# Products that nobody reads in TensorE's row, in the front of the first routed layer

## The reference

```
z = (x - mu) * rsqrt(var + EPS) * ln_g + ln_b          # layer norm of a layer norm of x
z_bn  = (mean over tokens of z - bn_mean) * rsqrt(bn_var + EPS) * bn_g + bn_b
probs = softmax(z_bn @ Wr + br);  idx = argmax(probs);  gate = probs[idx]     # one idx a sequence
h = relu(z @ W_down[idx] + b_down[idx])                # 128 -> 64
y = h @ W_up[idx] + b_up[idx]                          # 64 -> 128
x = x + y * gate
```

## Time and profile before

| | us |
|---|---|
| three runs | 1920.57, 1924.78, 1929.26 |
| median | 1924.78 |
| profiled execution, device time | 1917.87 |
| its span, first to last instruction | 1916.1 |
| outside the span | 1.8 |
| first routed layer's block | 266.6 to 322.6 of the span |

### The profile page before, as it was taken

One profiled execution on the slowest core, in us unless ns is written; L12 is line 12 of the kernel. 1 busy time (PEld: TensorE's weight loads), 2 busy tenths in 40 slices (PEclk: granted clock), 3 DMA queues, 4 the chain that ended last, 5 costly groups with the idle time before them and its releaser, 6 DMA issues. The chain is left out here.

```text
span 1916.1 us, 26161 instructions
## 1 busy us (share of the span) xinstructions
PE 1569.3 (82%) x8251; PEld 1048.2 (55%) x8251; DVE 1270.2 (66%) x2824; ACT 898.6 (47%) x1679; POOL 203.6 (11%) x184
## 2 busy tenths in 40 slices
PE   6999979788799999788948999999999879857005
PEld 5777755555466666455636666566666445523004
DVE  4777774586576676567656665666665558677985
ACT  3655642576455555456623222232222167627752
POOL 2100010112000000111410000000000111010410
PEclk9999985699799999899979999999999969958557
DMA  4000000321000000142100000000000022100001
GB/s 157 1 1 0 0 1 3 121 51 34 1 1 1 0 0 1 37 159 58 42 1 0 1 1 1 1 0 0 1 1 0 3 63 51 34 1 0 0 0 44
DMA packets 23374, 41.71 MB, mean 22 GB/s; under 512 B 7709, under 2 KB 11165, under 8 KB 22238
## 3 DMA queue, kind: packets, MB, share of 16 engines
q1 hardware_dynamic: 23262, 40.32, 7.1%
HBM read 19.32 MB, written 2.10 MB: 11 GB/s over the span
## 5 line engine op out<-in xcount | busy, mean ns | idle before, releaser
L973 DVE TENSOR_REDUCE mP_a<-psY_a 128x8 f32<-128x512 f32 x192 | 128.0, 687 | 106.6 <-PE psY_a L811 106.3
L731 ACT ACTIVATE probs_a<-psX_a 128x512 f32<-128x512 f32 x192 | 108.9, 595 | 134.1 <-PE psX_a L838 133.5
L1726 ACT ACTIVATE xsh_f<-xs_f 128x512 fp32r<-128x512 f32 x120 | 75.8, 632 | 197.8 <-DVE xs_f L1979 197.7
L1979 DVE TENSOR_TENSOR xs_f<-xT_f,psR_f 128x512 f32<-128x512 f32 x128 | 86.9, 686 | 78.4 <-PE psR_f L1798 74.4
L1842 PE MATMUL psX_f<-xs_f,wo_f2w 128*128 128x512 f32 x256 | 128.6, 594 | 0.0
L2374 PE MATMUL ps_f<-wT_f,xq_f 128*128 128x128 f32 x192 | 24.3, 290 | 125.5 <-DVE xq_f L2395 125.5
L1979 DVE TENSOR_TENSOR xs_f<-aoT_f,psR_f 128x512 f32<-128x512 f32 x128 | 85.8, 685 | 61.7 <-PE psR_f L1798 61.4
L1506 DVE SCALAR_TENSOR_TENSOR g_f<-psU_f,cols_f1w,t_f 128x512 f32<-128x512 f32 (+1 forms) x104 | 77.9, 749 | 72.8 <-ACT t_f L1319 71.1
L811 PE MATMUL psY_a<-ks_a,xs_a 96*128 96x256 f32 x384 | 99.3, 362 | 18.6 <-DMA xs_a<-ql_a 17.3
L1401 PE MATMUL psO_f<-h_f,w_f1w 128*128 128x512 f32 (+1 forms) x208 | 107.6, 599 | 0.0
L1319 ACT ACTIVATE t_f<-psU_f,cols_f1w 128x512 f32<-128x512 f32 (+1 forms) x104 | 71.2, 684 | 76.4 <-PE psU_f L1385 76.4
(11 more groups left out here) (435 smaller groups left out, 4161.5 us busy)
## 6 DMA issues: line engine op xcount, KB each, us to landing
xs_a<-qh_a SPq DMA_DIRECT2D x192, 64.0 KB, 2.0
xs_a<-ql_a SPq DMA_DIRECT2D x96, 64.0 KB, 2.0
x_sb<-in_x SPq DMA_DIRECT2D x1, 2048.0 KB, 8.6
out<-x_sb SPq DMA_DIRECT2D x1, 2048.0 KB, 6.3
w_f1w<-in_F_w SPq DMA_DIRECT2D x2, 792.0 KB
ctxT<-in_ctxT SPq DMA_DIRECT2D x1, 1024.0 KB, 12.6
maskf_a<-in_mask SPq DMA_DIRECT2D x8, 128.0 KB, 2.2
maskf_a<-in_maskT SPq DMA_DIRECT2D x8, 128.0 KB, 2.6
```

Of the source, the lines that this page charges most:

```text
L731: nc.scalar.activation(probs[:, b % 2, g, :, :], psX[g % 2][:].rearrange("p (e t) -> p e t", e=2), ACT.Exp, scale=float(dv) ** -0.5).then_ ...
L973: nc.vector.tensor_reduce(mP[:, b % 2, h // 2, col:col + 8], psY[h % 2][:].rearrange("p (h k) -> p h k", h=8), axis=AX.X, op=ALU.max).then ...
L1726: nc.scalar.activation(xsh[:, e % RING, :], xs[:, e % RING, :], ACT.Copy).then_inc(s("x_high").sem, 1)
L1979: nc.vector.tensor_tensor(xs[:, e % RING, :], src, psR[e % 2][:], ALU.mult).then_inc(s("scaled").sem, 1)
```

## The change

A helper `keep_busy(n)` issues n products of `sel` (128 by 128 as the stationary operand, 128 by 512 as the moving one, fp32r) into a PSUM bank of its own, `psW`, the eighth. Nobody reads that bank, the products wait for nothing and tell nobody. They stand at four places of TensorE's row: 22 before the first group of transpositions, 2 before each of the seven others, 8 before the product of the logits, 14 after it: 58 in all. No other engine's row changes.

```diff
+        psW = ctx.enter_context(nc.psum_tensor("psW_f0", [P, T4], F32))
...
         def _(pe):
+            def keep_busy(n):
+
+                for _ in range(n):
+                    nc.tensor.matmul(psW[:], common["sel"][:, 0, :], common["sel"][:, 0:4, :], start=True, stop=True)
+            keep_busy(22)
             for i in range(ITERS):
+                if i:
+                    keep_busy(2)
                 pe.wait_ge(s("ln_out").sem, s("ln_out").at(i + 1))
                 pe.wait_ge(s("z_ready").sem, s("z_ready").at(BPI * (i - 1)))
...
                 ins.then_inc(s("ln_T").sem, 1)
+            keep_busy(8)
             pe.wait_ge(s("pool_steps").sem, s("pool_steps").at(3))
...
                 ins.then_inc(s("ffn_out").sem, 1)
+            keep_busy(14)
             for b in range(B + 2):
                 if b < B:
                     hidden(b)
```

## The result

The changed kernel took 1898.77 us in the median of six runs (1894.56 to 1908.72), the kernel before 1921.30 in six (1916.65 to 1929.26). The ratio is 0.9885, with a 95% interval of 0.9854 to 0.9917: faster, by 22 us or 1.2%, clear of the noise. The prediction had a gain of 16.6 us and a time of 1908 us, in a range from 1900 to 1926. The direction and the mechanism in the changed block came as forecast; the time lies 1.2 us outside the range, on the fast side. Over all 63 runs of the kernel before and all 23 of the changed one, the later repeats with them, the medians are 1921.8 and 1901.7 us, 20 us apart: the first six runs were a little on the lucky side. The profiled execution took 1897.90 us, 20.0 under that of the kernel before.

What follows compares the result with a forecast made beforehand. It took the loop to be bound by TensorE at half clock. Block -15.3, next layer's start -1.3 and the rest zero made -16.6 us, from 1924.78 to 1908 us; range 1900 to 1926, likeliest case 1901 to 1915.

Steps and rivals of the forecast that it cites:

- The loop is bound by TensorE at half clock: In the first routed layer's loop: rounds of 2.20 us fall to 1.25 at full clock, 12 rounds giving -11.4 us.
- The clock stays up in the front and the loop keeps it: Granted clock 1.00 from 266 to the block's end near 307 of the span; chance of the forecast 0.58.
- The products hide: The 58 products lie in TensorE's waits in the front, the first 22 ending 0.3 us late; front gains 1.3 us.
- The block: First routed layer: front -1.3, opening -1.0, loop rounds -11.4, end -1.6, in sum -15.3 us.
- opening up to hidden(3): From the first copy of weights to hidden(3), 4.22 us before: only hidden(2) and up(0) shrink, -1.0 us.
- Net -1.3: Start of the next attention layer: first four records -1.8 us at full clock, later transpositions losing some 0.4.
- the same work shifted by 16.6 us: Everything behind the next layer's start: same work, clock changes falling elsewhere on it, taken as zero.
- 4 us on either side: Margin for the clock's changes behind the block, about half of the 8.7 us between three runs of one kernel.
- the reference point: The sum was put to 1924.78 us, the median of the runs shown, giving 1908 us.
- Rival A: Clock falls in the loop's opening or soon behind, never rising before the loop ends; time 1922.5 us, chance 0.27.
- Rival B: Clock falls in the front, at 269, in spite of the products, which then delay it: +9 us, 1934; chance 0.07.
- Rival C: Loop holds, but the second attention layer gives back 6 us or more beyond the margin: 1916 us, chance 0.08.

## Why the prediction was right and where it was not

- **The loop is bound by TensorE at half clock.** Right. With the clock at 1.00 and nothing else changed in it, a round went from 2.20 to 1.22 us; 1.25 was taken, from 1.10 to 1.35.
- **The clock stays up in the front and the loop keeps it.** Right in all of the changed kernel's three profiles. The reason given for doubt was real: without the 14 it fell just ahead of the opening.
- **The products hide.** Right: front 1.34 us shorter (1.3 forecast), 0.3 us of the 22 uncovered as worked out.
- **The block.** 56.2 to 40.9 us is -15.4, forecast -15.3, and not by errors that cancel: front -1.3 (-1.3 forecast), opening up to hidden(3) -1.0 (-1.0), from there to the end of the last add -13.1 (-13.0).
- **The step that failed** is the next one: "Net -1.3", and behind it "the same work shifted by 16.6 us [...]: zero, with 4 us on either side". Its mechanism was right for the first records (-1.8 us), the term was too small. Where 1.3 us stood, the second attention layer's block gained 5.6 us in the first pair and 3.7 in the mean of the profiles above. It had 53 us at half clock before and 43 after: 10 us less at half clock went with 5.6 us less time. The forecast let the full clock act on the first records alone and put the rest of that front at nothing. With products in it the block's clock went to 0.96 and its time to 156.3, so TensorE is waited for in a good part of it. Why a high clock at the entry should act for longer than the opening is not shown: in the first pair the clock came back 43 us after the block's start and stayed for some 100 us, where before it took 52 us to come back so.
- **The second reason is the reference point.** I put the sum to the median of the three runs shown, 1924.78. Over six runs it was 1921.30, and 1921.8, 1923.3 and 1921.5 in three later groups of 17 to 21. From 1921.3 the same sum gives 1904.7. With 3.5 us from there and 2.4 from the attention layer, 1908 becomes 1902; the changed kernel's medians were 1898.8, 1901.2 and 1903.6. What is left of the first result's distance is as large as the medians of one kernel lie apart; the two later medians lie inside the range of 1900 to 1926.
- **The 4 us on either side** for what the clock does elsewhere was too little for one block of one execution: the third attention layer's block took 183.6 and 185.2 us before, 190.1, 190.2 and 188.8 after, the fourth's 161.8 and 162.2 against 156.8, 156.6 and 156.3. They nearly cancel here (+6.5 and -5.0). What the forecast lacked is that the length of such a block goes, by and large, with its time at half clock: in the ten profiles without products in the attention fronts, from 156.8 us with 28 at half clock to 165.8 with 53 in the second, from 183.6 with 24 to 196.4 with 56 in the third, from 156.3 with 27 to 164.6 with 52 in the fourth. Where the clock's changes fall was not forecast, and what sets it is open. The range has a slip too: the loop's bounds and the 4 us make 1903 to 1913, not 1901 to 1915.
- **Rival A** did not occur in the changed kernel but did, as described, in the profile without the 14; its block gained 1.3 us where 1.8 were put. **Rival B** was not brought about. **Rival C**, a loss behind the block, was the wrong way round in the second attention layer; the third did lose 6.5 us, and the fourth gave 5.0 back.

## What to carry to other kernels

Where TensorE is busy all the time and yet bound, look at the granted clock before the work: the same products took 2.20 us at 0.50 and 1.22 at 1.00, and 32 us of them did not bring the clock back. Dense products that nobody reads, put into waits that other engines set, with their count from the wait's length and the price at full clock, cost next to nothing (0.3 us here; the 14 at the end of the block, where there was no wait, cost 5.2), and the ones just ahead of the bound stretch do most (13 of 15 us with 14 of 58, in one profile). Take the size from the block and expect what lies behind it to move by several us, and put the sum to a median of more than three runs.

## What the runs showed of the hardware

- The loop's products (64 columns, or 65 rows) kept a clock of 1.00 for 20 us (286 to 306 in the changed kernel) and did not lift one of 0.50 in 34 us (286 to 320 in the kernel without the 14), with PE busy for 11.84 of 12.00 us in the first and 34.00 of 34.00 in the second. Under 14 dense products of 128x512 the clock did go from 0.50 to 1.00, in both profiles that have them at half clock: 5.5 us after their start where they stand alone ahead of the loop (at 288.4), 5.4 us where they stand at the block's end (at 328.3).
- Unused products of 32 columns kept the clock at 1.00 as those of 128 did (268 to 302 us in that profile), in the same time (22 in 5.25 us against 5.26).
- Transpositions alone raised the clock from 0.50 to 1.00: in the repeat of the kernel before, at 282.7 us, TensorE had had nothing else since 274.25; in the kernel with products in the attention fronts alone, at 278.0, nothing else since 270.97.
- The stationary and moving operands of these products are zeros and ones, mostly zeros, and the clock stayed at 1.00 with them (266.00 to 306.10 in the changed kernel).
- The same kernel's attention blocks differed by 0.4 to 2.9 us between executions, with different clock rows and the same instructions: the changed kernel's second took 160.2, 163.1 and 161.9 us, with a mean clock of 0.87, 0.86 and 0.86.
